# Loads of the query and key stacks issued from ScalarE's queue, three steps into each group, instead of from SyncE's

## The chip, the cores and the metric

The kernel runs on one core of a Trainium2 chip. Its time is the device time of one launch in microseconds. Before the change three runs gave 3085.34, 3088.26 and 3089.69 us, a median of 3088.26.

## What is computed

`x` holds 8 sequences of 1024 tokens with 256 features. Four residual blocks follow each other:

```
x = x + linear_attention(layernorm(x))       # 16 heads of 16, softplus features, running sums over tokens
x = x + gated_ffn(layernorm(x))              # h = tanh(x wo + c_final uo + bo); c_final from a scan over sequences
x = x + alibi_attention(layernorm(x))        # 16 heads, causal softmax(q k / 4 - slope * distance) v, then Wo
x = x + gated_ffn(layernorm(x))              # the same weights
```

The ALiBi attention is what the change touches. Its scores are a matmul of a query stack and a key stack. Each stack has the 16 features of a head in two bfloat16 parts, three rows for the bias and one or two rows for the row maximum: 51 rows (queries) or 53 rows (keys) of 1024 tokens.

## The kernel before, in words

The kernel has two phases. Phase 1 does linear attention and the first feed-forward block. Phase 2 does the ALiBi attention and the second feed-forward block; it takes the span from about 1140 us on. Each engine runs an instruction stream of its own, written out by hand, and waits on semaphores that the others raise.

In phase 2 all engines go through the same list of steps `s`. A stage `b` has 144 steps (`BATCH`), one stage for each sequence, numbered 0 to 7; stages -2, -1 and 8 fill and drain. A stage is four groups of 36 steps (`GROUP`), and a group `gg` is four heads of one sequence; `kk` is the step inside the group and `k` the step inside the stage. At step `s`:

- TensorE (`attend`, lines 663 to 703) makes one score tile for the row maximum of a later step (`s + 44`, `LEAD`, into the banks `scores`) and one score tile, turned, for step `s` itself (into the banks `turned_scores`). There are two banks of each. The turned tile of step `s` waits until ScalarE has taken the one of step `s - 2` (line 688).
- VectorE reduces the `scores` bank to a maximum (line 1176).
- ScalarE takes the exponential of the `turned_scores` bank (`exp_unit`, line 902).
- Every fourth step TensorE multiplies the probabilities with the values (line 719).
- Between these, `fill(2, b, k)` has the projections of sequence b + 1 (k = 1 to 44), the output projection, normalization and feed-forward of sequence b - 1 (k = 13 to 139), and the last step of the first feed-forward block of sequence b + 2. The last one goes so: SyncE loads the sequence `x_after_attention` into `x_for_attention` (`load_x1`, line 351) and, in four pieces, the product `x_times_wo` into `ffn_h` (`load_h`, line 359). GpSimd adds the state's part (line 1319). ScalarE takes the tanh (line 956) at k = 6, 8, 34 and 36, between the exponentials. GpSimd adds the result (line 1325).

The order of ScalarE's instructions is fixed: if one waits, the exponentials behind it wait too.

The query and key stacks go through memory off chip. `store_qk` (line 298) writes the parts of a sequence to `q_stack` and `k_stack`; `load_group(gg)` (lines 366 to 378) reads the four heads of a group back, with four transfers: two of 204 KB for the queries, two of 212 KB for the keys. On chip there is room for three groups. So `load_group(gg)` waits until TensorE has made the last turned tile of group gg - 3 (`ex_full`), and for an even group also until the stores are done. TensorE needs the group first for its maxima, which is from step kk = 28 of group gg - 2 on.

SyncE's order in a stage b of phase 2 (lines 435 to 474) is: load_group(4b + 2), load_x1(b + 2), load_h pieces 0 and 1, store_qk of blocks 0 and 1 of sequence b + 1, load_h pieces 2 and 3, the store of the residual, load_group(4b + 3), store_qk of blocks 2 and 3, the residual's load, the store of `x_after_ffn`, the stores of `x_times_wo` (`store_xw`), load_group(4b + 4), load_group(4b + 5). load_group(4b + 5) waits for step k = 108, and load_group(4b + 6) for the end of the stage; what SyncE has to do next stands behind them.

ScalarE issues one kind of transfer itself already: `send_max` (line 923) at kk = 31, four small transfers of the maxima into the query stacks.

Of the kernel before, what the change touches and what calls it, by code (L numbers as in the profile page):

```python
# [20 lines left out]
SLOT = 64  # L21
ROWS = 3 * HD
QROWS = ROWS + 3
KROWS = ROWS + 5
# [22 lines left out]
HEADS = 4  # L47
GROUP = HEADS * NU
GROUPS = H // HEADS
# [72 lines left out]
def mixer_kernel(nc, x, weights, cols, rows, key_rows, masks, out):  # L122
    with ExitStack() as ctx:
        def sb(name, shape, dt):
            return ctx.enter_context(nc.sbuf_tensor(name, shape, dt))
# [4 lines left out]
        sem = {}  # L130
# [21 lines left out]
        q_dram = nc.dram_tensor("q_stack", (2, H, KROWS, T), BF16, kind="Internal").ap()  # L152
        k_dram = nc.dram_tensor("k_stack", (2, H, KROWS, T), BF16, kind="Internal").ap()
# [18 lines left out]
        QS = sb("q_stacks", [P, 6, T], BF16)  # L172
        KS = sb("k_stacks", [P, 6, T], BF16)
# [70 lines left out]
        def tokens(t, b):  # L244
            return t[b].rearrange("(n p) d -> p n d", p=P)
# [14 lines left out]
        def batch_in(b):  # L260
            return 0 <= b < B
# [8 lines left out]
        def group_in(gg):  # L270
            return 0 <= gg < B * GROUPS
# [10 lines left out]
        def _(sp):  # L282
# [17 lines left out]
            def store_xw(b):  # L300
                for c in range(4):
                    sp.wait_ge(sem["xw_out"], w.next("xw_out"))
                    sp.dma_start(tokens(xw_dram, b)[:, 2 * c:2 * c + 2],
                                 XW[:, c % 2, :].rearrange("p (n d) -> p n d", n=2)
                                 ).then_inc(sem[f"xw_stored{c % 2}"], 16)
# [17 lines left out]
            def store_residual(phase, pb):  # L323
                sp.wait_ge(sem[f"x3_done{phase}"], 4 * (pb + 1))
                sp.dma_start(tokens(x1_dram, pb), XR[:, :, :]).then_inc(sem[f"x3_out{phase}"], 16)
# [18 lines left out]
            def load_x1(fb):  # L344
                if fb == 0:
                    sp.wait_ge(sem["ln_norm1"], 4 * norms_to(1, "ln1", B - 1))
                else:
                    sp.wait_ge(sem["x2_out"], 16 * fb)
                    sp.wait_ge(sem["ln_norm2"], 4 * norms_to(2, "ln1", fb - 1))
                sp.wait_ge(sem["x3_out1"], 16 * (fb + 1))  # L350
                sp.dma_start(XA[:, :, :], tokens(x1_dram, fb)).then_inc(sem["xa_full2"], 16)

            def load_h(fb, c):
                if 4 * fb + c >= 2:
                    sp.wait_ge(sem["h_added"], 4 * fb + c - 1)
                else:
                    sp.wait_ge(sem["phi_done"], 4 * B)
                sp.wait_ge(sem[f"xw_stored{c % 2}"], 16 + 2 * 16 * fb + 16 * (c // 2 + 1))
                sp.dma_start(XI[:, c % 2, :].rearrange("p (n d) -> p n d", n=2),
                             tokens(xw_dram, fb)[:, 2 * c:2 * c + 2]).then_inc(sem[f"hx_in{c % 2}"], 16)  # L360

            def store_qk(nb, r):
                sp.wait_ge(sem["pk_low"], 4 * nb + r + 1)
                store_block(nb % 2, r, parts_of(r), sem[f"pk_sent{r}"])

            def load_group(gg):
                bb, half = gg // GROUPS, gg % GROUPS // 2
                if gg >= 3:
                    sp.wait_ge(sem["ex_full"], GROUP * (gg - 2))
                if gg % 2 == 0:  # L370
                    for n in (2 * half, 2 * half + 1):
                        sp.wait_ge(sem[f"pk_sent{n}"], 48 * (bb + 1))
                at, h0 = 2 * (gg % 3), HEADS * (gg % GROUPS)
                for g in range(2):
                    for stack, dram, n in ((QS, q_dram, QROWS), (KS, k_dram, KROWS)):
                        sp.dma_start(stack[SLOT * g:SLOT * g + n, at:at + 2, :],  # L376
                                     dram[bb % 2, h0 + g:h0 + HEADS:2, 0:n, :].rearrange("h r t -> r h t")
                                     ).then_inc(sem[f"pk_in{gg % 3}"], 16)

            for b in range(-2, B + 1):  # L380
                if batch_in(b + 2) and b + 2:
                    load_x(b + 2)
# [42 lines left out]
            def load_final(b):  # L425
                free_for_final(b)
                sp.wait_ge(sem["x3_out2"], 16 * (b + 1))
                for n in range(2):
                    sp.wait_ge(sem[f"xw_stored{n}"], 16 + 2 * 16 * (B + b + 1))
                for half in range(2):  # L430
                    sp.dma_start(FW[b][half], by_rows(xw_dram, b, half)).then_inc(sem[f"fin_in{b}"], 16)
                    sp.dma_start(FX[b][half], by_rows(x1_dram, b, half)).then_inc(sem[f"fin_in{b}"], 16)

            sp.wait_ge(sem["w_split"], w.next("w_split", 2))
            for b in range(-2, B + 1):
                if batch_in(b):
                    load_group(GROUPS * b + 2)
                if batch_in(b + 2):
                    if b + 2:
                        load_x1(b + 2)  # L440
                    load_h(b + 2, 0)
                    load_h(b + 2, 1)
                if batch_in(b + 1):
                    store_qk(b + 1, 0)
                    store_qk(b + 1, 1)
                if batch_in(b + 2):
                    load_h(b + 2, 2)
                    load_h(b + 2, 3)
                if b == B:
                    for n in (3, 4, 5):  # L450
                        load_final(n)
                if batch_in(b - 1):
                    store_residual(2, b - 1)
                if b == B:
                    for n in (1, 6):
                        load_final(n)
                if batch_in(b):
                    load_group(GROUPS * b + 3)
                if batch_in(b + 1):
                    store_qk(b + 1, 2)  # L460
                    store_qk(b + 1, 3)
                if batch_in(b):
                    load_residual(2, b)
                if batch_in(b + 2):
                    sp.wait_ge(sem["h_added"], 4 * (b + 3))
                    sp.dma_start(tokens(x2_dram, b + 2), XA[:, :, :]).then_inc(sem["x2_out"], 16)
                if batch_in(b - 1):
                    store_xw(b - 1)
                if batch_in(b + 1):
                    load_group(GROUPS * (b + 1))  # L470
                    load_group(GROUPS * (b + 1) + 1)
                if b == B - 1:
                    for n in (0, 2):
                        load_final(n)
# [356 lines left out]
        def _(act):  # L831
# [65 lines left out]
            def exp_unit(s):  # L897
                unit = s // HEADS
                if unit >= 3 and s % HEADS == 0:
                    act.wait_ge(sem["probs_used"], unit - 2)  # L900
                act.wait_ge(sem["ex_full"], s + 1)
                nc.scalar.activation(PR[:, s % SLOTS, :], TB[s % 2][:, :], ACT.Exp).then_inc(sem["ex_taken"], 1)  # L902
# [14 lines left out]
            def send_max(gg):  # L917
                act.wait_ge(sem["mx_row"], gg + 1)
                r = 2 * (gg % 3)
                for g in range(2):  # L920
                    for n in range(2):
# [2 lines left out]
                            "a r (b c) -> a (r b) c", c=P), MR[at:at + 2 * NT, gg % 2, :]  # L924
                            ).then_inc(sem[f"mx_sent{gg % 2}"], 16)

            def qk_in(nb, r, c):
                n = 4 * nb + r
                if c == 0 and n >= 2:
                    act.wait_ge(sem["pk_low"], n - 1)  # L930
                    act.wait_ge(sem[f"pk_sent{(r - 2) % 4}"], 48 * ((n - 2) // 4 + 1))
                at = slice(c * CH, (c + 1) * CH)
                src = general_in()
                bias = (C_BK if r % 2 else C_BQ) + r // 2
                nc.scalar.activation(QK[:, r % 2, at], src, ACT.Identity, bias=COL[:, bias:bias + 1])
                nc.scalar.activation(QKP[0][:, r % 2, at], src, ACT.Identity,
                                     bias=COL[:, bias:bias + 1]).then_inc(sem["pk_raw2"], 1)
# [33 lines left out]
            for s in STAGES:  # L971
                n, j = s // CHUNK, s % CHUNK
# [6 lines left out]
            for s in STAGES:  # L979
                b, k = s // BATCH, s % BATCH  # L980
                gg, kk = s // GROUP, s % GROUP
                if 0 <= s < STEPS:
                    exp_unit(s)
                if kk == 21 and group_in(gg):
                    heads_out(gg, 0)
                if kk == 5 and group_in(gg - 1):
                    heads_out(gg - 1, 1)
                if kk == 30 and group_in(gg + 1):
                    max_rows(gg + 1)
                if kk == 31 and group_in(gg + 1):  # L990
                    send_max(gg + 1)
                fill(2, b, k)
# [512 lines left out]
```

## Time and profile before

| | |
|---|---|
| median of 3 runs | 3088.26 us |
| the profiled execution's own time | 3114.58 us |
| its span | 3112.8 us, at a mean granted TensorE clock of 0.895 |
| TensorE matmul busy | 2452.2 us, 79% |
| VectorE busy | 1715.9 us, 55% |
| ScalarE busy | 1292.4 us, 42% |
| GpSimd busy | 796.2 us, 26% |
| SyncE's DMA queue (q1) | 167.15 MB, 16.3% of 16 engines |
| ScalarE's DMA queue (q10) | 0.53 MB, 0.1% |

The profiled execution is 26.3 us (0.9%) above the median. A busy share is an average over stretches with different limits. An engine's time for issuing a transfer is not counted as busy; the timeline shows it in rows of its own, as SPq for SyncE and ACTq for ScalarE. In a timeline row "idle before" is how long the engine had nothing to do ahead of it, and whose work ended that.

### The profile page before, as it was taken

Reading aid. Unit: us, or ns where it says so; the run is one execution under the profiler, and the core shown is the slowest. Engines: PE = TensorE matmul, PEld = TensorE weight load, DVE = VectorE, ACT = ScalarE, POOL = GpSimd, SP = SyncE. Lnnn points to the kernel's source line nnn. Section 1 sums busy time; section 2 is a strip of 40 time slices with the busy share of each in tenths; the row PEclk is TensorE's granted clock in tenths of the full one; section 3 lists DMA queues with packets and bytes.
Section 4 is the critical chain, followed back from the end, with each engine's and each line's share of the span. In section 5 each row is a group of like instructions: output and inputs, shape, how many; then the busy total and the mean of one; then the engine's idle time right before and its main releaser. Section 6 shows DMA issues by size and latency. Waiting matters only on the chain.

```text
span 3112.8 us, 51191 instructions
## 1 busy us (share of the span) xinstructions
PE 2452.2 (79%) x21200; PEld 1179.1 (38%) x21200; DVE 1715.9 (55%) x3769; ACT 1292.4 (42%) x2087; POOL 796.2 (26%) x660
## 2 busy tenths in 40 slices
PE   1568887888878864488699799798797999998963
PEld 1346555565555532132232233232332333323232
DVE  4445555455554432467476476575664766666325
ACT  1322324323242222065455455454554555555523
POOL 2333132331321015322141241241421321212020
PEclk9788998989989976598899899899898999999976
DMA  2001011010010112121220220221211301201152
GB/s 86 28 15 56 15 42 35 21 55 15 28 35 11 39 61 63 67 80 53 60 95 15 73 84 18 74 77 37 75 60 41 103 32 48 70 19 55 59 189 108
DMA packets 127416, 170.95 MB, mean 55 GB/s; under 512 B 8864, under 2 KB 94880, under 8 KB 127184
## 3 DMA queue, kind: packets, MB, share of 16 engines
q1 hardware_dynamic: 123088, 167.15, 16.3%
q8 instruction: 167, 2.74, 0.4%
q10 hardware_dynamic: 4096, 0.53, 0.1%
q14 instruction: 65, 0.53, 0.1%
HBM read 91.11 MB, written 76.02 MB: 54 GB/s over the span
## 4 chain that ended last, share of the span: by engine, by line
PE 57%; DVE 13%; issue 8%; ACT 6%; POOL 6%; SPq 5%; DMA 3%; ACTq 1%; POOLq 0%; DVEq 0%
PE general L538 14%; PE scores L678 8%; PE general L524 7%; PE out_of_heads L719 7%; POOL ln L1367 3%; SPq L376 3%; DMA ffn_h<-x_times_wo 3%; PE general L513 3%; PE scores L658 3%; DVE maxima L1176 3%; PE scores L572 2%; PE general L505 2%; PE out_of_heads L614 2%; PE turned_scores L658 2%; PE out_of_heads L624 2%
## 5 line engine op out<-in xcount | busy, mean ns | idle before, releaser
L1176 DVE TENSOR_REDUCE maxima<-scores 128x1 f32<-128x512 f32 (+3 forms) x1536 | 802.6, 553 | 609.4 <-PE scores L658 305.9
L902 ACT ACTIVATE probs_turned<-turned_scores 128x512 f32<-128x512 f32 x1152 | 681.1, 600 | 638.6 <-PE turned_scores L658 344.7
L678 PE MATMUL scores<-k_stacks,q_stacks 51*128 51x512 bf16 (+3 forms) x1536 | 462.0, 344 | 104.8 <-DVE maxima L1176 58.3
L692 PE MATMUL turned_scores<-q_stacks,k_stacks 53*128 53x512 bf16 (+3 forms) x1536 | 454.4, 339 | 90.7 <-ACT probs_turned L902 88.4
L678 PEld LDWEIGHTS scores<-k_stacks,q_stacks 51*128 51x128 bf16 x1536 | 112.8, 94 | 506.0 <-issue 252.3
L524 PE MATMUL general<-w_high,ln_turned_high 128*128 128x256 bf16 x768 | 218.6, 285 | 33.0 <-DVE ln_turned_low L1116 26.9
L844 ACT ACTIVATE gate_tanhs<-general,feature_vectors 128x512 f32<-128x512 f32 x192 | 131.5, 685 | 266.6 <-PE general L538 254.1
L1367 POOL TENSOR_SCALAR ln<-x_for_attention,ln_mean_var,ln_rstd 128x256 f32<-128x256 f32 x128 | 158.9, 1252 | 259.3 <-DVEq L1259 259.3
L524 PE MATMUL general<-w_low,ln_turned_high 128*128 128x256 bf16 x768 | 218.2, 284 | 0.0
L524 PE MATMUL general<-w_high,ln_turned_low 128*128 128x256 bf16 x768 | 217.7, 283 | 0.0
L1019 DVE SCALAR_TENSOR_TENSOR gate_tanhs<-gate_tanhs,state_doubled 128x512 f32<-128x512 f32 x64 | 55.2, 863 | 265.7 <-ACT gate_tanhs L844 265.5
L1388 POOL TENSOR_TENSOR ln_low<-ln 128x512 bf16<-128x512 f32 x128 | 134.0, 1055 | 241.8 <-DVE ln L1158 241.8
L1310 POOL TENSOR_TENSOR state_low<-state_doubled,state_high 128x2048 bf16<-128x2048 f32 x16 | 65.2, 4073 | 499.7 <-ACT state_high L850 499.7
L1358 POOL CAST maxima_parts<-maxima 128x16 bf16<-128x16 f32 x64 | 10.6, 198 | 710.6 <-DVE maxima L1183 710.6
L658 PE MATMUL scores<-mask_scores,identity 128*128 128x256 bf16 (+1 forms) x640 | 171.3, 268 | 0.0
L658 PE MATMUL turned_scores<-mask_turned,identity 128*128 128x256 bf16 (+1 forms) x640 | 166.7, 260 | 0.0
L505 PE MATMUL general<-identity,ln 128*128 128x128 bf16 x512 | 52.3, 276 | 144.2 <-POOL ln_low L1388 144.2
L719 PE MATMUL out_of_heads<-probs_turned,values 128*17 128x512 f32 (+3 forms) x1536 | 161.5, 518 | 0.0
L719 PE MATMUL out_of_heads<-probs_turned,values_odd_and_heads_out 128*17 128x512 f32 (+3 forms) x1536 | 157.8, 508 | 0.0
L692 PEld LDWEIGHTS turned_scores<-q_stacks,k_stacks 53*128 53x128 bf16 x1536 | 112.4, 94 | 118.3 <-ACT probs_turned L902 100.8
L872 ACT COPY values_odd_and_heads_out<-out_of_heads 128x512 f32<-128x512 f32 x64 | 37.5, 586 | 269.8 <-PE out_of_heads L624 264.1
L538 PE MATMUL general<-state_high,w_low 128*128 128x512 bf16 x384 | 147.4, 384 | 0.0
(199 smaller groups left out, 4897.7 us busy)
## 6 DMA issues: line engine op xcount, KB each, us to landing
x_after_attention<-x_residual SPq DMA_DIRECT2D x16, 1024.0 KB, 4.5
x_times_wo<-x_wo_out SPq DMA_DIRECT2D x64, 256.0 KB, 2.1
k_stacks<-k_stack SPq DMA_DIRECT2D x64, 212.0 KB
q_stacks<-q_stack SPq DMA_DIRECT2D x64, 204.0 KB
x_for_attention<-in_x SPq DMA_DIRECT2D x8, 1024.0 KB, 5.3
x_residual<-in_x SPq DMA_DIRECT2D x8, 1024.0 KB, 5.3
x_for_attention<-x_after_attention SPq DMA_DIRECT2D x8, 1024.0 KB, 20.9
ffn_h<-x_times_wo SPq DMA_DIRECT2D x32, 256.0 KB, 6.8
```

The source lines that it names most:

```text
L505: mm = pe.transpose(bank[:, :].bitcast(BF16)[:, n * P:(n + 1) * P], src, ident[:, :])
L524: mm = pe.matmul(bank[:, n * D:(n + 1) * D], src[xp][:, k, at], W[wp][:, m, k, :], start=(i == 0), stop=(i == len(todo) - 1))
L538: mm = pe.matmul(bank[:, :], W[wp][:, m, k, e * P:(e + 1) * P], src[xp][:, k, c * CH:(c + 1) * CH], start=(n == 0), stop=(n == len(todo) - 1))
L658: return pe.matmul(pe_out, ident[:, :], m, start=False, stop=True)
L678: mx = pe.matmul(bank_s[:, first * P:(first + tiles) * P], QS[at:at + QROWS, r, i * P:(i + 1) * P], KS[at:at + QROWS, r, k0 * P:(k0 + tile ...
L692: ex = pe.matmul(bank_t[:, first * P:(first + tiles) * P], KS[at:at + KROWS, r, j * P:(j + 1) * P], QS[at:at + KROWS, r, i0 * P:(i0 + tile ...
L719: mm = pe.matmul(OB[half][32 * g:32 * g + HV, at:at + tiles * P], values[:, j, HV * h:HV * (h + 1)], PR[:, (HEADS * unit + g) % SLOTS, fir ...
L844: nc.scalar.activation(TG[:, g, :], bank, ACT.Tanh, bias=COL[:, at:at + 1], scale=1.0 if g == 2 else 0.5).then_inc(sem["gate"], 1)
L902: nc.scalar.activation(PR[:, s % SLOTS, :], TB[s % 2][:, :], ACT.Exp).then_inc(sem["ex_taken"], 1)
L1176: r = dve.tensor_reduce(MP[:, gg % 2, g, at:at + 1], max_bank[m][:, first * P:(first + tiles) * P], AX.X, ALU.max)
L1367: i = pool.tensor_scalar(XN[:, t, :], src[:, t, :], MV[:, which, t, 0:1], RS[:, which, t:t + 1], ALU.subtract, ALU.mult)
L1388: pool.tensor_tensor(pair(XL, c), pair(XN, c), top(pair(XN, c)), ALU.subtract).then_inc(sem[f"ln_low{phase}"], 1)
```

## The change

`load_group` moves from SyncE's stream to ScalarE's, with the same waits and the same four transfers. SyncE's three calls in each stage are gone. ScalarE calls it for groups 0 and 1 at steps -49 and -48, and from then on for group gg + 2 at step kk = 3 of group gg, behind that step's exponential. Thirty of the 32 groups are loaded in that way, while exponentials run.

```diff
@@ SyncE, phase 2
-            def load_group(gg):
-                ...
             for b in range(-2, B + 1):
-                if batch_in(b):
-                    load_group(GROUPS * b + 2)
                 if batch_in(b + 2):
                     if b + 2:
                         load_x1(b + 2)
...
-                if batch_in(b):
-                    load_group(GROUPS * b + 3)
                 if batch_in(b + 1):
                     store_qk(b + 1, 2)
                     store_qk(b + 1, 3)
...
-                if batch_in(b + 1):
-                    load_group(GROUPS * (b + 1))
-                    load_group(GROUPS * (b + 1) + 1)
@@ ScalarE, phase 2
+            def load_group(gg):
+                bb, half = gg // GROUPS, gg % GROUPS // 2
+                if gg >= 3:
+                    act.wait_ge(sem["ex_full"], GROUP * (gg - 2))
+                if gg % 2 == 0:
+                    for n in (2 * half, 2 * half + 1):
+                        act.wait_ge(sem[f"pk_sent{n}"], 48 * (bb + 1))
+                at, h0 = 2 * (gg % 3), HEADS * (gg % GROUPS)
+                for g in range(2):
+                    for stack, dram, n in ((QS, q_dram, QROWS), (KS, k_dram, KROWS)):
+                        act.dma_start(stack[SLOT * g:SLOT * g + n, at:at + 2, :],
+                                     dram[bb % 2, h0 + g:h0 + HEADS:2, 0:n, :].rearrange("h r t -> r h t")
+                                     ).then_inc(sem[f"pk_in{gg % 3}"], 16)
...
                 if 0 <= s < STEPS:
                     exp_unit(s)
+                if s in (-49, -48):
+                    load_group(s + 49)
+                elif kk == 3 and gg >= 0 and group_in(gg + 2):
+                    load_group(gg + 2)
                 if kk == 21 and group_in(gg):
                     heads_out(gg, 0)
```

## Rows read from the trace of the kernel before

**Rows 1.** Windows, steps 108 to 143 of stage 2: us, busy by engine, clock, DMA share.
```profile
1891.00:1937.00 46.00, 45.36 (x315) 13.82 (x317) 30.04 (x60) 25.22 (x45) 0.72 (x4) 1.00 0.06 20
```
**Rows 2.** Waits of the whole span: who waited for whom, total, times, longest.
```profile
PE turned_scores L692 <- ACT probs_turned L902: 88.4, 16, 17.4
```
**Rows 3.** Timeline of SyncE's queue at the start of stage 3: start, us, what.
```profile
1937.04 0.23 SPq L376 DMA_DIRECT2D q_stacks<-q_stack  x1
1937.32 0.36 SPq L376 DMA_DIRECT2D k_stacks<-k_stack  x1
1937.72 4.17 SPq L376 DMA_DIRECT2D q_stacks<-q_stack  x1
1941.94 3.17 SPq L376 DMA_DIRECT2D k_stacks<-k_stack  x1
1945.22 8.04 SPq L351 DMA_DIRECT2D x_for_attention<-x_after_attention  x1
```
**Rows 4.** Timeline of all engines, where the stall at k = 6 of stage 3 ends.
```profile
1966.88 2.48 POOL L1319 TENSOR_TENSOR ffn_h<-ffn_h,state_part_of_h 128x512 f32<-128x512 f32 x2 [22.93 <-DMA ffn_h<-x_times_wo]
1968.18 0.63 ACT L956 ACTIVATE ffn_h<-ffn_h 128x512 f32<-128x512 f32 x1 [19.54 <-POOL ffn_h L1319]
1969.35 0.60 PE L692 MATMUL turned_scores<-q_stacks,k_stacks 53*128 53x512 bf16 x1 [16.43 <-ACT probs_turned L902]
```
**Rows 5.** Timeline of SyncE's queue: k = 36 of stage 3, k = 0 and 36 of stage 6.
```profile
2012.11 0.26 SPq L376 DMA_DIRECT2D q_stacks<-q_stack  x1
...
2595.84 0.23 SPq L376 DMA_DIRECT2D q_stacks<-q_stack  x1
...
2651.90 0.24 SPq L376 DMA_DIRECT2D q_stacks<-q_stack  x1
```
**Rows 6.** Timeline of GpSimd in stage 2: the last normalization of sequence b + 2.
```profile
1860.33 2.43 POOL L1367 TENSOR_SCALAR ln<-x_for_attention,ln_mean_var,ln_rstd 128x256 f32<-128x256 f32 x2
```
**Rows 7.** Timeline of ScalarE in stage 2 around its own four transfers, kk = 31.
```profile
1785.47 0.60 ACT L902 ACTIVATE probs_turned<-turned_scores 128x512 f32<-128x512 f32 x1 [0.64 <-PE turned_scores L658]
1785.48 2.43 ACTq L923 DMA_DIRECT2D q_stacks<-maxima_rows  x4
1788.03 0.69 ACT L935 ACTIVATE qk_block<-general,feature_vectors 128x512 f32<-128x512 f32 x1 [1.97 <-issue]
```
**Rows 8.** Timelines of ScalarE and TensorE, stage 2: exponential k = 111, turned tile k = 114.
```profile
1896.24 0.60 ACT L902 ACTIVATE probs_turned<-turned_scores 128x512 f32<-128x512 f32 x1
...
1899.69 0.33 PE L692 MATMUL turned_scores<-q_stacks,k_stacks 53*128 53x384 bf16 x1
```
**Rows 9.** Timeline, stage 3: exponential k = 3, copy k = 4, projection k = 5.
```profile
1942.32 0.62 ACT L902 ACTIVATE probs_turned<-turned_scores 128x512 f32<-128x512 f32 x1
...
1944.61 1.01 ACT L895 COPY ln_turned_low<-general 128x1024 bf16<-128x1024 bf16 x1
...
1946.55 0.38 PE L513 MATMUL general<-ln_turned_high,w_high 128*128 128x512 bf16 x1 [1.43 <-DVE ln_turned_low L1116]
```
**Rows 10.** Timelines, stage 2: exponentials k = 38 and 39, tiles of k = 42.
```profile
1797.04 1.24 ACT L902 ACTIVATE probs_turned<-turned_scores 128x512 f32<-128x512 f32 x2
...
1803.12 0.33 PE L678 MATMUL scores<-k_stacks,q_stacks 51*128 51x384 bf16 x1 [1.01 <-DVE maxima L1176]
```
**Rows 11.** A short idle of TensorE (timeline), and the window behind it.
```profile
1645.36 0.39 PE L678 MATMUL scores<-k_stacks,q_stacks 51*128 51x512 bf16 x1 [2.23 <-DVE maxima L1176]
```
**Rows 12.** Windows: just behind that idle, and while three groups load.
```profile
1646.00:1648.00 2.00, 2.00 (x16) 0.48 (x18) 1.19 (x2) 1.01 (x2) 0.00 (x0) 0.50 0.00 0
...
1290.00:1300.00 10.00, 8.61 (x23) 1.90 (x21) 8.74 (x14) 0.00 (x0) 0.00 (x0) 0.50 0.12 40
```
**Rows 13.** Timelines where attention starts: ScalarE's last work, SyncE's first load, TensorE's first tiles.
```profile
1251.57 0.69 ACT L936 ACTIVATE qk_high<-general,feature_vectors 128x512 bf16<-128x512 f32 x1
...
1259.82 1.14 SPq L376 DMA_DIRECT2D q_stacks<-q_stack  x1
...
1289.42 0.61 PE L678 MATMUL scores<-k_stacks,q_stacks 51*128 51x512 bf16 x2 [33.47 <-DMA k_stacks<-k_stack]
```

More of the change, by code:

```diff
@@ L364, in store_qk @@
                 store_block(nb % 2, r, parts_of(r), sem[f"pk_sent{r}"])
-            def load_group(gg):
[L367 to L378, printed above, removed]
             for b in range(-2, B + 1):
```

## The prediction

> **What bounds the kernel now.** I read the waits first, then the timeline of one stage, then windows. In the steps without disturbance TensorE has no slack: it is busy for 45.36 of 46 us in steps 108 to 143 of a stage, at full granted clock, and a step there lasts 46/36 = 1.28 us [rows 1]. Whatever stops TensorE in such a stretch is paid in full.
>
> The list of waits has one wait of TensorE that stands out: 88.4 us on the exponentials, in 16 pieces, the longest 17.4 us [rows 2]. Five of the 16 are longer than 16 us, one in each of the stages 1 to 5, and together they are nearly all of it. The timeline shows where such a piece comes from. At the start of stage 3 SyncE issues the four loads of a group; it then needs 8.04 us for the load of `x_for_attention`, and only behind that come the loads of `ffn_h` [rows 3]. GpSimd waited 22.93 us for these, ScalarE 19.54 us for GpSimd at k = 6, with the next exponential behind the tanh, and TensorE 16.43 us for that exponential [rows 4]. When it resumes, its matmul of 512 columns takes 0.60 us, where those at full clock take 0.38 [rows 4, 9]: the granted clock is at the lower of its two levels, 1.2 GHz against 2.4.
>
> **What the change takes away.** With the group loads gone, SyncE meets load_x1(b + 3) right behind the stores of `x_times_wo`, and the last thing that load waits for is the normalization of the sequence now in the buffer. GpSimd ends it at 1862.8 [rows 6], 74 us ahead of the stage's end at 1937.04 [rows 3]. The loads of `ffn_h` are then on chip long before step 6, and the wait goes. What is late next at k = 6: GpSimd's split of the state at the stage's end and two sums; my reading of the order is that they end before ScalarE comes there, because ScalarE itself is now held at k = 3.
>
> Its worth: steps 0 to 36 last 2012.11 - 1937.04 = 75.1 us in stage 3, and 2651.90 - 2595.84 = 56.1 in stage 6, which has no `ffn_h` to load [rows 3, 5]. The difference, 19.0 us, is the 16.43 of idle time and 2.6 us of matmuls at the lower clock. Five stages give 5 x 19.0 = 95 us. Stage 0 has a wait at k = 6 too, worth about 1 us.
>
> At the start of the attention TensorE waits 33.47 us for the first group; SyncE issues it at 1259.82, behind stores, while ScalarE has been free since 1252.3 [rows 13]. On ScalarE it is issued 7.5 us earlier, but beside those stores rather than behind them. I take 8 us with the better order behind it; bounds 0 and 12. Sum of the gains: 95 + 1 + 8 = 104 us.
>
> **What it adds.** Thirty times ScalarE issues four loads between two exponentials. On SyncE these four take 0.23, 0.36, 4.17 and 3.17 us, 8.1 us from the first's start to the last's end [rows 3]. The queue was empty at the first; the third and fourth are held back while the earlier ones drain. A group has 2 x (204 + 212) = 832 KB and flows at 40 GB/s while nothing else does [rows 12], so it needs 20.8 us: the engine that issues it cannot get rid of it at once. ScalarE's queue is as empty at kk = 3 as SyncE's was, since its own four small transfers are from the group before. I take 8.1 us. The bounds from rows: 2.43 us, what ScalarE's four small transfers take [rows 7], and 8.1.
>
> Does an issue hold the exponentials? ScalarE's own transfers say yes: they start 0.01 us behind the start of an exponential, so they run beside it, but the next instruction starts only at 1788.03, 0.1 us behind their end, with 1.97 us of idle time that nothing but the issue explains [rows 7]. So the exponential of kk = 4 starts 8.2 us behind that of kk = 3.
>
> TensorE's cover is two banks: tiles 4 and 5 can be made, tile 6 needs exponential 4.
> - Steps k = 75 and 111 (14 loads; 7 each, as groups 30 and 31 start none): exponential 3 starts at 1896.24, tile 6 at 1899.69 [rows 8]. Afterwards exponential 4 starts at 1904.4 and ends at 1905.0, tile 6 starts at 1905.1. Stall 5.4 us; 14 x 5.4 = 76 us.
> - Step k = 3 (8 loads): the projection at k = 5 needs ScalarE's copy at k = 4. Exponential 3 starts at 1942.32; exponential 4 at 1950.5, the copy of 1.01 us at 1951.0, so the projection starts at 1952.1 in place of 1946.55 [rows 9]. Stall 5.5 us; 8 x 5.5 = 44.
> - Step k = 39 (8 loads): exponential 3 starts at 1797.7, tile 6 would come at 1806.6 in place of 1803.12 [rows 10]: 3.4 us. Below it, VectorE is behind there (1.01 us of wait in that row) and catches up during the stall, so 1.6; above it, the stores of blocks 2 and 3 now run beside the loads and can hold the issue longer, as the backlog held load_x1 for 8.04 us [rows 3], so 8. I take 3.4, nearest to the rows; 8 x 3.4 = 27.
>
> Issue stalls: 76 + 44 + 27 = 147 us.
>
> Then the clock. TensorE resumes at half clock behind a stall of 16.43 us, and an idle time of 2.23 us already ended in one, with 0.50 in the window behind it [rows 4, 11, 12]. A stall of 5.4 us lies between. I price its tail as that of the long one, 2.6 us, rounded to 2.5: 22 x 2.5 = 55. The eight shorter ones, where VectorE sets part of the pace, get 1 us: 8. Together 63; bounds 0 and 30 x 2.6 = 78.
>
> **What is added and costs nothing.** The transfers themselves are hidden: issued at kk = 3, needed at kk = 28, which is 25 x 1.28 = 32 us later plus the stall, against 21 us of flow. If that cover went (a flow at half speed, 42 us), each load would cost some 5 to 10 us more. SyncE is freed of 32 x 8 us of issuing, which no engine waits for beyond what is counted above. VectorE and GpSimd get no work.
>
> **Sum.** 147 + 63 - 104 = +106 us. The profiled execution took 3114.58 us (span 3112.8), 26 above the median. The terms are differences inside it; put on the median, 3088 + 106 = 3194.
>
> The Trainium skill speaks against what a second queue could bring: transfers started from ScalarE and SyncE end up on the same 16 engines, and only the sequencer's time of starting them is saved, "usually small relative to the DMA itself" (DMA: Bandwidth & Descriptors, Issuing engines are not separate DMA queues). Here that time is 8.1 us against 20.8 of flow [rows 3, 12], so the trace doesn't agree that it is small, and it is moved onto an engine on the path. Were it small, the result would be that of the first rival below.
>
> **Rivals.**
> *ScalarE's queue takes the loads at once (faster, chance 0.12).* The 7.3 us of the third and fourth issue could be SyncE's own backlog and not the shape's. If the four cost 2.43 us, as ScalarE's small ones [rows 7], exponential 4 ends at 1896.24 + 2.55 + 0.6 = 1899.4, before tile 6 at 1899.69, and TensorE never stops; at k = 3 the copy ends at 1946.5 against 1946.55. All 104 us of gain stay: 2984. It decides below about 2.8 us for the four; half way, near 5 us, the stalls are some 2.3 x 30 = 69 us and the sum is still below zero without a clock loss. Against it: SyncE's queue had been idle before 1937.04 and still stuck at the third. The Trainium skill has a rule that leans the same way (DMA: Bandwidth & Descriptors, Why a DMA increments its semaphore by 16 and not by 1): a transfer is spread over the largest number up to 16 that divides its slowest dimension, so 51 rows go to 3 engines and 53 to one, whichever queue they come from. The 40 GB/s agree with few engines.
>
> *Stalls but no clock loss (0.17).* 147 - 104 = +43: 3131. For it: TensorE is busy right up to a stall and right behind it. Against it: 2.23 us of idle time were enough for 0.50 in the window behind [rows 11, 12].
>
> *The gain doesn't come (0.06).* If something else holds load_x1 or the tanh at k = 6, only 9 us of the 104 stay: +201, 3289. Against it stand the 74 us between GpSimd's last read and the stage's end.
>
> *Costs and gains cancel (0.04).* An issue of about 5.5 us with little clock loss: within a few us of 3088.
>
> **How the numbers follow.** Forecast 0.61: 3194, its own range from no loss at k = 39 beyond the 1.6 and a clock loss of half (3088 + 133 + 31 - 108 = 3144) to all upper bounds (3088 + 184 + 78 - 96 = 3254). With the case of no clock loss at its lower end (3088 + 133 - 108 = 3113) the range is 3110 to 3256; 2 in 10 lie outside. Faster by more than 0.2% (6 us, about what can be told here): 0.14; within: 0.02; slower: 0.84.
>
> **What the changed kernel's profile would show.** ACTq rows for `q_stacks` and `k_stacks` at kk = 3, the third and fourth of 3 to 4 us. TensorE's wait for the exponentials in some 30 pieces of 3 to 6 us, none of 16. No idle time ahead of the tanh at k = 6. Steps 108 to 143 at about 46 + 8 = 54 us, and a granted clock below 1.00 there. Steps 0 to 36 of stage 3 near 56 + 8 = 64. First tile of the attention near 1281. I am wrong if the four issues take under 3 us, if the stall at k = 6 is still there, or if the granted clock stays full through the stalls.

## The result and the profile after

Four runs of the changed kernel took 3225.88 to 3234.28 us, median 3230.14. Beside them four runs of the kernel before had a median of 3088.98 us. The ratio is 1.0425, with a 95% interval of 1.0384 to 1.0465: slower by 141 us, inside the predicted range of 3110 to 3256, 36 us above the predicted time. The profiled execution took 3232.46 us, with a span of 3230.6 us and a mean granted clock of 0.875 (0.895 before). Lines have moved by the edit: the exponential is L881 now, the turned tile L671, the group's loads L916.

The first view is the list of TensorE's waits over the span of the changed kernel (who waited for whom: total us, times, longest).

```profile
PE turned_scores L671 <- ACT probs_turned L881: 139.8, 34, 10.6
...
PE general L492 <- ACT ln_turned_low L874: 48.1, 7, 7.1
PE scores L657 <- DVE maxima L1173: 43.8, 85, 1.0
PE scores L657 <- DMA k_stacks<-k_stack: 32.5, 1, 32.5
```

The 88.4 us of before [rows 2], most of it in five long pieces, have become 139.8 + 48.1 = 188 us, none of whose pieces reaches 11 us. In the timeline thirty of them, of 4.5 to 10.6 us, stand behind the thirty groups that are loaded between exponentials. They sum to 184 us.

Three of the four places, in stage 2 and 3, from the timelines of ScalarE, TensorE and SyncE (start, us, engine, line, what, idle before it). First k = 111, which answers to [rows 8]:

```profile
1932.94 0.25 ACTq L916 DMA_DIRECT2D q_stacks<-q_stack  x1
1933.08 0.60 ACT L881 ACTIVATE probs_turned<-turned_scores 128x512 f32<-128x512 f32 x1
1933.23 0.37 ACTq L916 DMA_DIRECT2D k_stacks<-k_stack  x1
1933.63 4.57 ACTq L916 DMA_DIRECT2D q_stacks<-q_stack  x1
...
1938.23 2.57 ACTq L916 DMA_DIRECT2D k_stacks<-k_stack  x1
1940.90 1.09 ACT L881 ACTIVATE probs_turned<-turned_scores 128x512 f32<-128x512 f32 x2 [7.22 <-issue]
...
1941.56 0.61 PE L671 MATMUL turned_scores<-q_stacks,k_stacks 53*128 53x384 bf16 x2 [4.64 <-ACT probs_turned L881]
```

The third and fourth issue are the long ones, as on SyncE [rows 3]; ScalarE's next exponential starts 0.1 us behind the last; the tile waits for it.

At k = 3 of stage 3, the place of [rows 9]:

```profile
1987.43 0.25 ACTq L916 DMA_DIRECT2D q_stacks<-q_stack  x1
...
1987.80 0.62 ACT L881 ACTIVATE probs_turned<-turned_scores 128x512 f32<-128x512 f32 x1
...
1996.16 0.60 ACT L881 ACTIVATE probs_turned<-turned_scores 128x512 f32<-128x512 f32 x1 [7.74 <-issue]
1996.65 1.01 ACT L874 COPY ln_turned_low<-general 128x1024 bf16<-128x1024 bf16 x1
...
1997.71 0.61 PE L492 MATMUL general<-ln_turned_high,w_high 128*128 128x512 bf16 x1 [7.11 <-ACT ln_turned_low L874]
...
2000.79 0.62 ACT L949 ACTIVATE ffn_h<-ffn_h 128x512 f32<-128x512 f32 x1
```

The last of these rows is the tanh at k = 6: it has no idle time ahead of it, where before it had 19.54 us [rows 4].

At k = 39 of stage 3, which answers to [rows 10] (those are of stage 2):

```profile
2052.08 0.25 ACTq L916 DMA_DIRECT2D q_stacks<-q_stack  x1
2052.36 0.44 ACTq L916 DMA_DIRECT2D k_stacks<-k_stack  x1
2052.83 8.30 ACTq L916 DMA_DIRECT2D q_stacks<-q_stack  x1
...
2053.78 1.18 SPq L298 DMA_DIRECT2D k_stack<-qk_high  x2
...
2061.16 3.44 ACTq L916 DMA_DIRECT2D k_stacks<-k_stack  x1
2064.70 1.08 ACT L881 ACTIVATE probs_turned<-turned_scores 128x512 f32<-128x512 f32 x2 [12.03 <-issue]
...
2065.35 0.60 PE L671 MATMUL turned_scores<-q_stacks,k_stacks 53*128 53x384 bf16 x2 [7.45 <-ACT probs_turned L881]
```

The third issue takes 8.30 us, twice as long as elsewhere, while SyncE's stores run. In the other stages it takes 7.1 to 9.4 us at this place, except in stage 7, where SyncE has no such stores: there it takes 4.69 us.

SyncE now loads for the sequence after next long before the stage's end (its timeline, in stage 2; stage 3 starts near 1984):

```profile
1894.22 0.36 SPq L351 DMA_DIRECT2D x_for_attention<-x_after_attention  x1
1894.68 2.21 SPq L359 DMA_DIRECT2D ffn_h<-x_times_wo  x2
```

And the windows from the issue at k = 111 to that at k = 3, and from there to that at k = 39 (us, busy by engine, clock, DMA share, GB/s):

```profile
1932.94:1987.43 54.49, 48.98 (x319) 15.24 (x318) 30.06 (x60) 26.94 (x47) 3.28 (x5) 0.91 0.05 17
1987.43:2052.08 64.65, 54.79 (x425) 23.15 (x421) 38.24 (x89) 35.91 (x64) 18.30 (x16) 0.92 0.22 69
```

The 46 us of [rows 1] are 54.5 for as many steps. TensorE's busy time rose by 3.6 us for the same work, at a clock of 0.91 in place of 1.00.

### The profile page after: what moved, and what is told of

Read it like the earlier page. It is cut to its first block, busy times and chain, and to the rows that moved or that the text cites. A ratio compares the mean times of both kernels' runs of the same rounds, so it can differ in the third digit from the quotient of the medians.

```text
span 3230.6 us, 51191 instructions
## 1 busy us (share of the span) xinstructions
PE 2507.3 (78%) x21200; PEld 1188.6 (37%) x21200; DVE 1706.9 (53%) x3769; ACT 1291.2 (40%) x2087; POOL 795.1 (25%) x660
## 4 chain that ended last, share of the span: by engine, by line
PE 60%; DVE 10%; ACTq 9%; issue 8%; ACT 7%; POOL 3%; DMA 2%; SPq 0%; POOLq 0%; DVEq 0%
PE general L517 13%; PE scores L657 9%; ACTq L916 8%; PE out_of_heads L698 8%; PE general L503 7%; PE general L492 4%; PE scores L637 3%; PE scores L551 2%; DVE maxima L1173 2%; PE turned_scores L637 2%; PE general L484 2%; PE out_of_heads L593 2%; PE out_of_heads L603 2%; PE turned_scores L671 2%; ACT probs_turned L881 2%
## 5 line engine op out<-in xcount | busy, mean ns | idle before, releaser
L881 ACT ACTIVATE probs_turned<-turned_scores 128x512 f32<-128x512 f32 x1152 | 678.5, 599 | 867.0 <-PE turned_scores L637 313.6
L671 PE MATMUL turned_scores<-q_stacks,k_stacks 53*128 53x512 bf16 (+3 forms) x1536 | 469.1, 350 | 140.6 <-ACT probs_turned L881 139.8
L657 PE MATMUL scores<-k_stacks,q_stacks 51*128 51x512 bf16 (+3 forms) x1536 | 473.1, 353 | 89.5 <-DVE maxima L1173 43.8
L1355 POOL CAST maxima_parts<-maxima 128x16 bf16<-128x16 f32 x64 | 10.6, 196 | 864.7 <-DVE maxima L1180 864.7
L1016 DVE SCALAR_TENSOR_TENSOR gate_tanhs<-gate_tanhs,state_doubled 128x512 f32<-128x512 f32 x64 | 44.2, 690 | 265.9 <-ACT gate_tanhs L823 265.7
L671 PEld LDWEIGHTS turned_scores<-q_stacks,k_stacks 53*128 53x128 bf16 x1536 | 113.6, 95 | 172.1 <-ACT probs_turned L881 156.6
L637 PE MATMUL turned_scores<-mask_turned,identity 128*128 128x256 bf16 (+1 forms) x640 | 176.0, 275 | 0.0
L698 PE MATMUL out_of_heads<-probs_turned,values 128*17 128x512 f32 (+3 forms) x1536 | 172.2, 547 | 0.0
L492 PE MATMUL general<-ln_turned_high,w_high 128*128 128x512 bf16 x256 | 104.1, 407 | 65.1 <-ACT ln_turned_low L874 48.1
```

The source lines that it names most:

```text
L492: mm = pe.matmul(bank[:, :], W[wp][:, m, k, e * P:(e + 1) * P], src[xp][:, k, c * CH:(c + 1) * CH], start=(n == 0), stop=(n == 5))
L637: return pe.matmul(pe_out, ident[:, :], m, start=False, stop=True)
L657: mx = pe.matmul(bank_s[:, first * P:(first + tiles) * P], QS[at:at + QROWS, r, i * P:(i + 1) * P], KS[at:at + QROWS, r, k0 * P:(k0 + tile ...
L671: ex = pe.matmul(bank_t[:, first * P:(first + tiles) * P], KS[at:at + KROWS, r, j * P:(j + 1) * P], QS[at:at + KROWS, r, i0 * P:(i0 + tile ...
L698: mm = pe.matmul(OB[half][32 * g:32 * g + HV, at:at + tiles * P], values[:, j, HV * h:HV * (h + 1)], PR[:, (HEADS * unit + g) % SLOTS, fir ...
```

## The experiments

**The gain alone.** If the stall at k = 6 comes only from SyncE's order, exchanging two entries there must bring it, with all loads left on SyncE.

```diff
-                if batch_in(b):
-                    load_group(GROUPS * b + 2)
                 if batch_in(b + 2):
                     if b + 2:
                         load_x1(b + 2)
                     load_h(b + 2, 0)
                     load_h(b + 2, 1)
+                if batch_in(b):
+                    load_group(GROUPS * b + 2)
```

> The kernel before, with one exchange in SyncE's order: load_x1 and the first two load_h of sequence b + 2 stand ahead of load_group(4b + 2) instead of behind it. All loads stay on SyncE. Theory (the gain and the cost of the change are two separate things, and the gain is only the five stalls at k = 6): TensorE's waits of 16 to 17 us go, no others come, 3089 - 5 x 18.3 = about 2997 us. Rival (the gain needs the group loads off SyncE's queue, since they share its rings with the other transfers): the stalls shrink by the 8 us of the group's issue at most, 3089 - 40 = about 3049 or more.

Measured: 3002.21 us, 0.9687 of the kernel before on that chip (0.9642 to 0.9732; before 3102.19). The five stalls are gone, and no wait for exponentials is left among TensorE's longest (ahead of these rows stands one wait for GpSimd, 141.7 us, 144.2 before; of the rows, the second and third belong to phase 1):

```profile
PE scores L678 <- DVE maxima L1176: 57.8, 94, 2.2
PE out_of_heads L614 <- DVE probs_turned L1123: 56.9, 14, 6.0
PE scores L572 <- issue: 49.6, 35, 1.7
PE scores L678 <- DMA k_stacks<-k_stack: 33.5, 1, 33.5
```

So the gain at k = 6, 98.7 us by the ledger below, has nothing to do with ScalarE's queue, and the cost can be read against this kernel. ScalarE's copies out of `out_of_heads` at kk = 5 and 21 are marks that every kernel has; the spacing of their starts gives a ledger of the profiled executions, in us over the whole span:

| place of the load (from the mark before it to the second mark behind it) | changed kernel less this one | TensorE's stalls there | predicted, with clock |
|---|---|---|---|
| around k = 3 (7 stages) | 53.8 | 46.2 | 56 |
| around k = 39 (8) | 71.8 | 61.9 | 35 |
| around k = 75 (7) | 36.1 | 36.0 | 55 |
| around k = 111 (7) | 55.8 | 33.2 | 55 |
| up to the first mark, with stage 0's k = 3 | 4.6 | 6.9 | |
| sum | 222.1 | 184.2 | |

222.1 us is the difference of the two spans, 3230.6 and 3008.5. Phase 1, whose code is the same, took equally long in both (its last matmul into `scores` starts at 1089.3 and 1088.9 us). The same ledger for the kernel before against this one has 17.4 to 21.2 us in each of the five intervals with the stall at k = 6, 98.7 in all.

**The same loads in pairs.** Three experiments vary how long ScalarE is held, with the same data on the same queue.

```diff
-                elif kk == 3 and gg >= 0 and group_in(gg + 2):
-                    load_group(gg + 2)
+                elif kk in (3, 11) and gg >= 0 and group_in(gg + 2):
+                    load_group(gg + 2, (kk // 8,))      # one query and one key load each
```

> The changed kernel, but ScalarE issues a group's four loads as two pairs, one query and one key load at kk = 3 and the others at kk = 11. Same loads, same bytes, same queue. Theory (what costs is that the third and fourth issue wait for the first two transfers to drain, and ScalarE stands still meanwhile): every pair takes 0.6 to 0.7 us, inside the 2.8 us that TensorE's two banks cover, the thirty stalls go and the time falls from 3230 to about 3000. Rival (moving this much data through ScalarE's queue while exponentials run costs by itself, in whatever portions): the 14 us of issuing per two groups are only spread, thirty stalls become sixty shorter ones, above 3150.

Measured: 3023.04 us (0.9774, 0.9724 to 0.9824), 207 us under the changed kernel's 3230.14. The expectation's phrase of 14 us should have been 8 us of issuing for each group. Each pair is short, here from the start of stage 3 in ScalarE's timeline, and the exponentials run on:

```profile
1898.45 0.25 ACTq L916 DMA_DIRECT2D q_stacks<-q_stack  x1
1898.73 0.38 ACTq L916 DMA_DIRECT2D k_stacks<-k_stack  x1
...
1900.62 0.60 ACT L881 ACTIVATE probs_turned<-turned_scores 128x512 f32<-128x512 f32 x1 [1.18 <-PE turned_scores L637]
```

TensorE's waits for exponentials fall to 6.6 us. What remains above 3002 is another thing, TensorE waiting for groups that have not landed:

```profile
PE scores L657 <- DMA k_stacks<-k_stack: 51.8, 10, 32.7
...
PE turned_scores L671 <- ACT probs_turned L881: 6.6, 12, 2.2
```

Beyond the first group's wait of 32.7 these are 19 us in nine pieces: the second pair starts 8 steps later, and its cover was thinner than the 25 steps of a load at kk = 3. The rival, above 3150 us, is out.

**Three and one.**

```diff
-                    load_group(gg + 2)
+                    load_group(gg + 2, (0, 1, 2) if kk == 3 else (3,))      # kk in (3, 11)
```

> The changed kernel, with three of a group's four loads issued at kk = 3 and the last key load alone at kk = 11. Theory (TensorE's two banks cover about 2.8 us of issuing, and what is longer is paid in full, with the matmuls at the lower clock behind it): the three take 0.25 + 0.4 + 4.2 = 4.9 us, TensorE stalls about 2 to 3 us thirty times, 60 to 90 us above the variant with two and two (3023), plus up to 2.5 us of clock each: 3090 to 3170 us. Rival (a stall of a few microseconds is worked off later, only the long one counts): within 15 us of 3023.

Measured: 3108.74 us (1.0045 of before, 1.0014 to 1.0076), 86 us above the pairs. TensorE's waits for ScalarE in this kernel:

```profile
PE turned_scores L671 <- ACT probs_turned L881: 67.8, 34, 6.7
...
PE general L492 <- ACT ln_turned_low L874: 25.4, 7, 3.9
```

93 us of stalls and 86 us of time, which the rival (within 15 us) can't give. The stalls differ by place: 1.6 to 2.1 us at k = 75 and 111 in all stages but the first, where ScalarE is held for about 5 us, 2.9 to 3.9 at k = 3, and 3.0 to 6.7 at k = 39, where SyncE's stores run beside the third issue again and ScalarE is held for 8.1 to 10.0 us (5.4 in stage 7). In the mean of all loads the pairs, three and one, and the unaltered four give stalls of about 0, 3.1 and 6.1 us, and times of 3023, 3109 and 3238 us (the last is the repeat of the changed kernel, below). The first step is paid about in full. The second costs 129 us for 91 us more of stalls; a part of the rest is a difference in phase 1, shown further on.

**The same data in another shape.** Each load is cut by rows into 48 and the rest, eight issues in place of four. (TensorE waits for twice the count; that line is left out here.)

```diff
-                        act.dma_start(stack[SLOT * g:SLOT * g + n, at:at + 2, :], ...)
+                        for r0, r1 in ((0, ROWS), (ROWS, n)):                  # ROWS = 48
+                            act.dma_start(stack[SLOT * g + r0:SLOT * g + r1, at:at + 2, :], ...)
```

> The changed kernel, with each of the four loads cut by rows into 48 rows and the remaining 3 (queries) or 5 (keys): eight issues at kk = 3 in place of four. Theory (the shape of the transfers makes them slow: 51 and 53 rows spread over few DMA engines, so they drain at 40 GB/s and hold the issuer): 48 rows spread over all engines, each issue takes 0.3 to 0.6 us, about 3.5 us for the eight, so TensorE stalls 0.5 to 1 us thirty times, and the first group lands some 20 us earlier: 2980 to 3030 us. Rival (what holds the issue is a price per transfer on a queue with two or more in flight): eight issues hold ScalarE for about 16 us, and the time rises above 3400 us.

Measured: 2986.14 us (0.9631, 0.9592 to 0.9669): 244 us under the changed kernel, with the loads at the same place in ScalarE's order. Eight issues take 2.8 us (ScalarE's timeline in stage 2), and 3.1 to 5.4 us at k = 39, beside SyncE's stores (2.8 in stage 7, without them):

```profile
1868.04 0.68 ACTq L917 DMA_DIRECT2D q_stacks<-q_stack  x2
1868.74 0.69 ACTq L917 DMA_DIRECT2D k_stacks<-k_stack  x2
1869.47 0.67 ACTq L917 DMA_DIRECT2D q_stacks<-q_stack  x2
1870.16 0.69 ACTq L917 DMA_DIRECT2D k_stacks<-k_stack  x2
```

TensorE's first tile of the attention comes at 1256.95 in place of 1285.32, with phase 1 equally long. Where nothing else moves, a whole group flows in 6 us in place of some 23, here as windows over this load and over the changed kernel's at k = 111 (the last two figures are the share of the 16 DMA engines and GB/s):

```profile
1868.00:1874.00 6.00, 4.36 (x53) 2.29 (x47) 3.19 (x7) 3.51 (x6) 4.49 (x3) 1.00 0.70 142
1933.00:1954.00 21.00, 16.36 (x106) 5.04 (x98) 7.37 (x17) 6.84 (x13) 0.00 (x0) 0.84 0.10 37
```

So it was the shape. Cut at 48 rows, the same bytes leave ScalarE free in a third of the time. The busy share goes from 0.10, the work of one or two of 16 engines, to 0.70, that of eleven.

**The place k = 39, first try.** Where does the third issue's 8.3 us come from? Moved past the stores:

```diff
-                elif kk == 3 and gg >= 0 and group_in(gg + 2):
+                elif kk == (11 if gg % GROUPS == 1 else 3) and gg >= 0 and group_in(gg + 2):
```

> The changed kernel, with the load issued at k = 39 of each stage moved to k = 47, behind the stores of the query and key blocks; the other three stay at kk = 3. Theory (the 12.7 us that ScalarE is held at k = 39, against 8.1 elsewhere, come from SyncE's stores of the same steps on the same DMA engines): the issue there takes 8 us, TensorE's stall falls from 7.5 to about 4.5 us, eight times 3 to 4 us: about 3202 us. Rival (the stall at k = 39 is long because of what the engines have to do in those steps, whatever the transfers): 3230 within its noise of 4 us.

Measured: 3238.53 us (runs from 3229.45 to 3260.02), no better; the expected 30 us did not come. The timeline at k = 47 of stage 2 says why it tells less than it should:

```profile
1816.86 4.36 ACTq L916 DMA_DIRECT2D q_stacks<-q_stack  x1
...
1820.83 0.37 SPq L321 DMA_DIRECT2D x_residual<-x_after_ffn  x1
1821.25 4.22 ACTq L916 DMA_DIRECT2D k_stacks<-k_stack  x1
...
1826.22 0.60 PE L671 MATMUL turned_scores<-q_stacks,k_stacks 53*128 53x256 bf16 x2 [6.04 <-ACT probs_turned L881]
...
1848.59 0.39 PE L657 MATMUL scores<-k_stacks,q_stacks 51*128 51x512 bf16 x1 [3.09 <-DMA k_stacks<-k_stack]
```

The third issue is back at 4.36 us, as the theory has it (4.4 to 5.1 in the stages 1 to 7), but now the fourth takes 4.22 us, beside SyncE's load of the residual, and the stall is 6.0 us (5.8 to 9.6 over the stages). Five groups issued this late are also not there when TensorE wants them, 8.6 us in all. The run moved several things at once and can't tell the theory from its rival.

**The place k = 39, second try.** Hold SyncE's stores instead and leave ScalarE alone.

```diff
+                if batch_in(b) and batch_in(b + 1):
+                    gg = GROUPS * b + 3
+                    sp.wait_ge(sem[f"pk_in{gg % 3}"], 64 * (gg // 3 + 1))
                 if batch_in(b + 1):
                     store_qk(b + 1, 2)
```

> The changed kernel, with SyncE's stores of query and key blocks 2 and 3 held until the group that ScalarE loads from k = 39 on has landed. ScalarE's order is as in the changed kernel. Theory (at k = 39 the issue takes 12.7 us in place of 8.1 because SyncE's stores move at the same time): the third issue there falls from 8.3 to 8.7 us to about 4.2, TensorE's stall from 7.5 to about 3.4 us, seven times some 4 us: 28 us less than the unaltered changed kernel. Rival (the long stall belongs to what the engines compute in those steps): issue and stall stay, and so does the time, within 5 us.

Beside it the changed kernel ran again, unaltered: 

> The changed kernel once more, unaltered, on the chip of the next three, so that they have something to stand beside: about 3235 us. No theory hangs on it.

Measured: 3215.55 us (1.0371, 1.0329 to 1.0414) against 3237.91 for the changed kernel (1.0427, 1.0375 to 1.0478). The medians differ by 22 us, but the intervals overlap, and the profiled executions differ by 17 us before the first group is even loaded, in phase 1, where the code is the same. These are ScalarE's first load and the window from 300 to 900 us, first in the unaltered kernel (e5), then in this one:

```profile
1249.89 0.51 ACTq L916 DMA_DIRECT2D q_stacks<-q_stack  x1
300.00:900.00 600.00, 498.10 (x5729) 339.59 (x5722) 312.42 (x713) 206.15 (x275) 169.63 (x101) 0.89 0.10 31
1232.58 0.51 ACTq L919 DMA_DIRECT2D q_stacks<-q_stack  x1
300.00:900.00 600.00, 489.50 (x5861) 332.10 (x5854) 326.82 (x753) 213.72 (x285) 171.92 (x104) 0.93 0.10 31
```

The granted clock is 0.89 in one and 0.93 in the other. So the medians decide nothing here, and the trace has to carry this one. At k = 39 of stage 2:

```profile
1800.72 4.37 ACTq L919 DMA_DIRECT2D q_stacks<-q_stack  x1
...
1805.12 2.56 ACTq L919 DMA_DIRECT2D k_stacks<-k_stack  x1
...
1808.43 0.60 PE L674 MATMUL turned_scores<-q_stacks,k_stacks 53*128 53x384 bf16 x2 [2.58 <-ACT probs_turned L884]
```

The stall is 2.58 us where the changed kernel has 7.55; over the eight stages the third issue takes 4.4 to 4.8 us and the stalls are 2.6 to 5.7, 3.5 in the mean. In the ledger the interval before the mark at k = 41 costs 35.9 us in place of 69.5. SyncE's stores are what doubles the third issue. A part of the gain was paid back elsewhere: the held stores push the stores of `x_times_wo` back, ScalarE waited 3.83 us for one of these and TensorE for ScalarE, and the interval before k = 77 costs 63.5 us in place of 39.3. From the first mark on the ledger has 207 us, against 218 and 227 in the two profiled executions of the changed kernel: 11 to 21 us are won, less than the 28 expected.

```profile
1843.62 0.59 ACT L961 COPY x_wo_out<-general 128x512 f32<-128x512 f32 x1 [3.83 <-DMA x_times_wo<-x_wo_out]
...
1844.90 0.60 PE L660 MATMUL scores<-k_stacks,q_stacks 51*128 51x512 bf16 x1 [3.67 <-ACT maxima_rows L896]
```

**Both mends, nothing on ScalarE.**

> The kernel before, with both mends and no load on ScalarE: load_x1 and load_h ahead of load_group(4b + 2) on SyncE, and each load cut into 48 rows and the rest. Theory (the gain of the order and the gain of the shape add, and nothing is left to pay on ScalarE): the order's 3002, less about 28 us for the first group landing in some 6 us in place of 31, so about 2973 us, 10 us under the kernel that issues the same cut loads on ScalarE (2986). Rival (with loads this short it doesn't matter who issues them): 2986 within 5 us.

Measured: 2984.35 us (0.9629, 0.9596 to 0.9662), 3.7% faster than the kernel before, and 7.8% faster than the changed one's 3237.91 on the same chip. It is level with the cut loads on ScalarE (2986.14), so the rival stands: with issues of about 3 us for a group, these runs show no difference between the two engines. The 28 us expected beyond the reordering came as 18 in the medians; in the profiled executions TensorE waits 16.2 us for the first group in place of 33.5, and the rest of their difference of 35 us is phase 1, of the shorter kind here.

## Why the prediction was right

*What bounds the kernel* held: TensorE has no slack in most of a stage, and most stops are paid; where VectorE holds it up a few steps on, a stop is paid in part (k = 75, below). *The gain* held: 95 for the five stalls at k = 6, measured 98.7. The start gave 4 us in place of 8 (first tile at 1285.32, before at 1289.42), and 1.5 us of these are a difference in phase 1: the first load was issued 12 us earlier, but its group took 37.5 us to be there, not 29.6. The likely reason is the one that the prediction gave for its bound, that the loads now run beside SyncE's stores; no run separates it. The order alone, predicted at 96 us, is 104.3 between the two spans and 100 between the medians.

*The issue holds the exponentials* held, with both its numbers: 0.1 us from the last issue's end to the next exponential, and third and fourth issues of 2.6 to 4.7 us where nothing else moves. One detail was off: at k = 3, 75 and 111 of most stages the first issue starts 0.06 to 0.37 us ahead of the exponential written before it; at k = 39 it starts 0.01 behind, as predicted.

*The stalls* were put at 147 us and are 184. At k = 75 and 111 they are 5.1 and 4.7 us (5.4 predicted), at k = 3 mostly 6.7 to 7.1 (5.5; TensorE had waited 1.43 us for VectorE at that place before, which is now inside the stall). The term that was mis-sized is k = 39: 3.4 predicted, 7.7 measured. The prediction named the reason and the bound (stores beside the loads, up to 8 us) and took the lower value, "nearest to the rows"; holding the stores gave 3.5 us in the mean, the predicted 3.4, so the cause is shown. By cost this place has 72 us where 35 were forecast.

*The clock* was put at 63 us. Cost less stalls in the ledger is 222 - 184 = 38 us, which mixes the clock with work that gets done during a stall. At k = 111 it is 3.2 us for each load, above the 2.5 predicted; at k = 75 nothing. There, in five stages of the kernel with the order alone, TensorE waits 2.2 us for VectorE a few steps later [rows 11] and runs at 0.93 of the clock from k = 77 to 93. In the changed kernel VectorE catches up during the stall and that wait is gone, while the clock in those steps is 0.87 to 0.90: what the one costs the other gives back. The prediction counted such catching up at k = 39 alone. The two errors, -37 and +25, leave the cost 12 us short: 210 predicted, 222 measured. That the sum came so close is partly luck.

*The rest of the 36 us* is the base. In the profiled executions the change costs 117.8 us (106 predicted); in the medians 141. In both of these executions phase 1 was of the longer kind (its last matmul into `scores` starts at 1090.8 before and 1089.3 after; the shorter kind, five of the ten profiled executions, has it at 1070 to 1073). The profiled execution of before took 26 us more than the median of its neighbours, that of the changed kernel 2 us more. My reading is that the neighbours of the first had the short phase 1 and those of the second the long one, so that some 18 us of the 141 are not the change's. The unprofiled runs have no trace that could show it, and whether the change itself makes the long kind more frequent stays open. The prediction's step of adding a difference from inside one execution to the median took a clock loss as common to both kernels that the kernel before has only in some of its runs.

*The rivals.* ScalarE's queue taking the loads at once is out, and the shape experiment shows that it would have been right with other row counts; its threshold of 2.8 us is borne out by eight issues of 2.8 us behind which TensorE's waits for exponentials sum to 6.1 us, none over 0.9, and those for its copy to 7.5 (48.1 in the changed kernel). The case without clock loss is out by the granted clock of 0.91 in the window of the result, 1.00 before, and by the 3.2 us for each load at k = 111. The gain came, so the third is out, and so is the fourth. The Trainium skill's sentence that the sequencer's share is "usually small relative to the DMA itself" (DMA: Bandwidth & Descriptors, Issuing engines are not separate DMA queues) did not hold for these loads, 8.1 us beside a flow of some 23, nor for the cut ones, 2.8 us beside 6. The Trainium skill's rule on how a transfer is spread (the same page, Why a DMA increments its semaphore by 16 and not by 1) gives, as my estimate, all 16 engines for 48 rows, 3 for 51 and 1 for 53. It agrees with 142 against 37 GB/s and with busy shares of 0.70 and 0.10; which engines each load used the views don't tell.

## What to carry to other kernels

In this kernel ScalarE was not free until a transfer had been handed over, and how long that took hung on the transfer's shape and on what else was moving. So read it from the queue's rows before moving an issue onto an engine on the path, and compare it with what the buffers between the engines cover. When a load is late, look first at what stands ahead of it in its queue's order. Exchanging two entries brought here what moving 128 loads brought; cutting 53 rows into 48 and 5 brought 28 us more at the start of the attention, and took away nearly all that the move had cost. And before a small difference is put down to an edit, compare a part of the two traces that the edit doesn't touch.

## What the runs showed of the hardware

- A group's loads of 51 and 53 partitions flowed at about 37 to 40 GB/s where nothing else moved (some 23 us, busy share 0.10 of the DMA engines); the same rows cut at 48 at 142 GB/s (6 us, busy share 0.70), from the same queue.
- With two such loads in flight, the third issue mostly takes 4.0 to 5.1 us, on SyncE as on ScalarE, and 7.1 to 9.4 us while the other queue stores 1.5 MB. The first two take 0.25 and about 0.4 us while exponentials run, seldom more.
- An exponential behind the four issues starts 0.1 us after the end of the last; the one ahead of them runs beside the first.
- The same phase 1 took 18 us more in five of ten profiled executions than in the others, with a granted clock of 0.89 against 0.93 from 300 to 900 us in the two shown. Of the kernel before, the run of 3087.01 us had a mean clock of 0.906, the one of 3093.54 had 0.905, and the one of 3114.78 had 0.895. What decides which it is, no run shows.
